# Two halves of queries instead of one block: the score, exp and value steps of an attention loop in a fused transformer block

## The reference

```python
Q, K = _rope(Q, K)
K = jnp.repeat(K, G, axis=1)
V = jnp.repeat(V, G, axis=1)
scores = jnp.einsum('bhqd,bhkd->bhqk', Q, K) / np.sqrt(HD)
w = jax.nn.softmax(scores, axis=-1)
attn = jnp.einsum('bhqk,bhkd->bhqd', w, V)
...
x = x + _L0_attn_ref(xn, ...) + _L0_ffn_ref(xn, ...)
```

## Time and profile before

| | |
|---|---|
| Time, median of 3 runs | 4692.35 us (4692.27 to 4919.59) |
| Time of the profiled execution | 4691.55 us |
| Its span on the slowest core (core 2) | 4690.0 us |
| Spans of the eight cores | 4655.5 to 4690.0 us |
| TensorE busy | 3501.9 us (75% of the span) |
| ScalarE busy | 1244.2 us (27%) |
| VectorE busy | 902.2 us (19%) |
| First and last exp of the attention start at | 1219.7 and 3020.2 us |

### The profile page before, as it was taken

The page is one execution under the profiler, slowest core; times in us unless marked ns, Lnnn a source line. Parts: engine busy times, 40 slices in busy tenths (PEclk is TensorE's granted clock), DMA queues, the critical chain, the costliest instruction groups (busy, mean ns, idle before and its releaser), DMA issues.

```text
span 4690.0 us, 35554 instructions; the slowest of 8 cores (4655.5 to 4690.0 us)
## 1 busy us (share of the span) xinstructions
PE 3501.9 (75%) x13728; PEld 1223.5 (26%) x13898; DVE 902.2 (19%) x1009; ACT 1244.2 (27%) x1100; POOL 224.4 (5%) x428
## 2 busy tenths in 40 slices
PE   3646555555777777777777777759998895999898
PEld 0212111111211111111111111124443342444344
DVE  3242333333111111111111111120000002000000
ACT  1010111111455555555555555500000000000000
POOL 0000000000000000000000000001110000111000
PEclk9878766666888888888888888879999997999999
DMA  5242443433000000000000000079998877999887
GB/s 104 41 90 50 75 87 84 83 79 79 5 0 0 0 0 0 0 0 0 0 0 0 0 0 0 1 143 153 152 150 156 161 142 143 152 153 152 158 161 142
DMA packets 95332, 340.02 MB, mean 72 GB/s; under 512 B 10784, under 2 KB 10816, under 8 KB 90688
## 3 DMA queue, kind: packets, MB, share of 16 engines
q0 software_dynamic: 60608, 274.81, 35.4%
q1 hardware_dynamic: 34560, 62.93, 4.6%
HBM read 604.07 MB, written 8.39 MB: 131 GB/s over the span
## 4 chain that ended last, share of the span: by engine, by line
PE 46%; ACT 22%; DVE 13%; DMA 12%; issue 5%; DVEq 0%; POOL 0%; ACTq 0%; another core or an unknown queue 0%; SPq 0%; POOLq 0%
ACT ptab L450 20%; PE pb L604 9%; PE pb L594 9%; PE pb L438 6%; DMA wo_sb<-wo_t 6%; PE pb L295 6%; PE pb L641 6%; DMA xf_sb<-x_t 3%; PE pb L347 3%; DVE rz_sb L499 2%; DVE rz_sb L501 2%; PE pb L636 2%; DMA xf<-x_t 1%; DVE scrf L273 1%; DVE xt_sb L276 1%
## 5 line engine op out<-in xcount | busy, mean ns | idle before, releaser
L450 ACT ACTIVATE ptab<-pb,negb_sb 128x2048 bf16<-128x2048 f32 x512 | 1007.1, 1967 | 795.3 <-PE pb L438 795.3
L594 PE MATMUL pb<-xt,wg_sb 128*128 128x512 bf16 x2008 | 471.0, 382 | 99.6 <-DVE xt L575 56.6
L438 PE MATMUL pb<-qt_all,kt_all 64*128 64x512 bf16 x2048 | 328.7, 396 | 211.5 <-ACT ptab L450 210.8
L604 PE MATMUL pb<-xt,wu_sb 128*128 128x512 bf16 x2006 | 464.2, 382 | 2.6 <-issue 0.2
L641 PE MATMUL pb<-gated,wd_sb 128*128 128x512 bf16 x2009 | 445.2, 379 | 2.1
L476 PE MATMUL pb<-ptab,v_all 128*64 128x512 bf16 x1024 | 420.8, 411 | 3.0 <-DVE pb L423 3.0
L482 PE MATMUL pb<-ptab,ones_bf 128*1 128x512 bf16 x1024 | 392.3, 383 | 0.0
L610 ACT ACTIVATE silu_sb<-pb 128x512 bf16<-128x512 f32 x128 | 76.4, 597 | 1182.9 <-PE pb L594 1182.8
L499 DVE RECIPROCAL rz_sb<-pb 1x1024 f32<-1x1024 f32 x16 | 104.8, 6551 | 1431.1 <-PE pb L482 1431.1
L295 PE MATMUL pb<-xt_sb,wk_sb 128*128 128x512 bf16 x496 | 204.4, 545 | 213.4 <-DVE xt_sb L276 212.9
L463 PE MATMUL pb<-ptab,v_all 128*65 128x512 bf16 x1024 | 327.2, 402 | 6.0 <-ACT ptab L450 6.0
(11 more groups left out here) (97 smaller groups left out, 1840.2 us busy)
## 6 DMA issues: line engine op xcount, KB each, us to landing
wg_sb<-wg_t POOLq DMA_DIRECT2D x128, 512.0 KB, 6.4
wu_sb<-wu_t POOLq DMA_DIRECT2D x128, 512.0 KB, 6.4
wd_sb<-wd_t POOLq DMA_DIRECT2D x32, 2048.0 KB, 16.0
xf_sb<-x_t SPq DMA_DIRECT2D x128, 256.0 KB, 2.7
xt_sb<-x_t POOLq DMA_DIRECT2D x32, 512.0 KB, 16.0
wk_sb<-wk_t POOLq DMA_DIRECT2D x32, 512.0 KB, 6.9
wq_sb<-wq_t POOLq DMA_DIRECT2D x32, 512.0 KB, 5.5
wo_sb<-wo_t POOLq DMA_DIRECT2D x32, 512.0 KB, 19.5
```

The source lines that it names most:

```text
L438: last = em.emit("tensor", (lambda p, j, c, h, base, off: lambda t: t.matmul(pscore[:, off:off + 512], kt_all[base:base + 64, 4096 * p + 1 ...
L450: exp_ab[c] = em.emit("scalar", (lambda par: lambda s: s.activation(ptab[:, 2048 * par:2048 * (par + 1)], pscore[:, :], AF.Exp, bias=negb_ ...
L594: mg = em.emit("tensor", (lambda par, dc: lambda t: t.matmul(pg[par][:, :], wg_sb[:, 2048 * par + 128 * dc:2048 * par + 128 * (dc + 1)], x ...
L604: mu_ = em.emit("tensor", (lambda par, dc: lambda t: t.matmul(pu[par][:, :], wu_sb[:, 2048 * par + 128 * dc:2048 * par + 128 * (dc + 1)], ...
```

## The change

The unit of the loop becomes one half of the queries (`h`) of a chunk, for both heads. `S_half(c, h)` issues two matmuls, one for each head, into a half of `pscore`, and waits for the exp of the same half of the chunk before. `EXP(c, h)` handles 128 x 1024 scores. `AV(c, h)` issues one A, one B and one O. To keep the two heads of one half side by side, the columns of `pscore` and `ptab` are laid out half first, head second, instead of head first. The tokens `exp_ab`, `s_ab`, `av_a`, `av_b` and `prev_pair_exp` are kept for each half. The end of a pair is as before, except that the first reciprocal names one token, where it named two.

```diff
-        def S_quad(c):
-            w_s = [a_ready, a_ready_sc, negb_tok, exp_ab.get(c - 1)]
+        if j == 0:
+            prev_pair_exp = {}
+
+        def S_half(c, h):
+            w_s = [a_ready, a_ready_sc, negb_tok, exp_ab.get((c - 1, h))]
             if j > 0 and c == 0:
-                w_s.append(prev_pair_exp)
+                w_s.append(prev_pair_exp.get(h))
...
-                    base = 64 * hh
-                    off = 1024 * hh + 512 * h
...
+            for hh in range(2):
+                base = 64 * hh
+                off = 1024 * h + 512 * hh
...
+                    waits=(w_s if hh == 0 else []),
+                    inc=(S_PE if hh == 1 else None))
+            s_ab[(c, h)] = last
+
+        def EXP(c, h):
             par = c % 2
-            w_e = [s_ab[c], av_b.get(c - 2)]
-            exp_ab[c] = em.emit("scalar", (lambda par: lambda s: s.activation(
-                ptab[:, 2048 * par:2048 * (par + 1)], pscore[:, :], AF.Exp,
-                bias=negb_sb[:, :], scale=0.125))(par), waits=w_e, inc=S_SC)
-
-        def AV(c, hh):
+            w_e = [s_ab[(c, h)], av_b.get((c - 2, h))]
+            exp_ab[(c, h)] = em.emit("scalar", (lambda par, h: lambda s: s.activation(
+                ptab[:, 2048 * par + 1024 * h:2048 * par + 1024 * (h + 1)],
+                pscore[:, 1024 * h:1024 * (h + 1)], AF.Exp,
+                bias=negb_sb[:, :], scale=0.125))(par, h), waits=w_e, inc=S_SC)
+
+        def AV(c, h):
...
+            pt_a = ptab[:, 2048 * par + 1024 * h:2048 * par + 1024 * h + 512]
+            pt_b = ptab[:, 2048 * par + 1024 * h + 512:2048 * par + 1024 * (h + 1)]
+            w_av = [exp_ab[(c, h)]]
+            if first and h == 0:
+                w_av.append(prev_evac)
+            av_a[(c, h)] = em.emit("tensor", (lambda c, p, h, first, last, pt_a: lambda t: t.matmul(
+                pava[0:65, 512 * h:512 * (h + 1)],
...
+            w_b = [bmemset] if (first and h == 0) else []
...
+            av_b[(c, h)] = em.emit("tensor", (lambda c, h, pt_b: lambda t: t.matmul(
+                pavb[0:1, 512 * h:512 * (h + 1)], ones_bf[:, 0:1],
+                pt_b, start=False, stop=False, skip_group_check=True))(c, h, pt_b),
+                inc=S_PE)
 
         for c in range(NKCH):
-            S_quad(c)
-            EXP(c)
-            if c >= 1:
-                AV(c - 1, 0)
-                AV(c - 1, 1)
+            for h in range(2):
+                S_half(c, h)
+                EXP(c, h)
+                if c >= 1:
+                    AV(c - 1, h)
         AV(NKCH - 1, 0)
         AV(NKCH - 1, 1)
-        av_final = av_b[NKCH - 1]
-        prev_pair_exp = exp_ab[NKCH - 1]
+        av_final = av_b[(NKCH - 1, 1)]
+        prev_pair_exp = {h: exp_ab[(NKCH - 1, h)] for h in range(2)}
...
-                     waits=[av_a[NKCH - 1], av_final])
+                     waits=[av_final])
```

More of the change, by code:

```diff
@@ L427, in build_nc @@
         s_ab = {}
-        def S_quad(c):
-            w_s = [a_ready, a_ready_sc, negb_tok, exp_ab.get(c - 1)]
+        if j == 0:
+            prev_pair_exp = {}
+        def S_half(c, h):
+            w_s = [a_ready, a_ready_sc, negb_tok, exp_ab.get((c - 1, h))]
             if j > 0 and c == 0:
-                w_s.append(prev_pair_exp)
+                w_s.append(prev_pair_exp.get(h))
             last = None
-            for h in range(2):
-                for hh in range(2):
-                    base = 64 * hh
-                    off = 1024 * hh + 512 * h
[L438 to L445, removed]
@@ L447, in EXP @@
-        def EXP(c):
-            par = c % 2
-            w_e = [s_ab[c], av_b.get(c - 2)]
-            exp_ab[c] = em.emit("scalar", (lambda par: lambda s: s.activation(
-                ptab[:, 2048 * par:2048 * (par + 1)], pscore[:, :], AF.Exp,
-                bias=negb_sb[:, :], scale=0.125))(par), waits=w_e, inc=S_SC)
-        def AV(c, hh):
+            for hh in range(2):
+                base = 64 * hh
+                off = 1024 * h + 512 * hh
+                last = em.emit("tensor", (lambda p, j, c, h, base, off: lambda t: t.matmul(
+                    pscore[:, off:off + 512],
+                    kt_all[base:base + 64, 4096 * p + 128 * c:4096 * p + 128 * (c + 1)],
+                    qt_all[base:base + 64, TOK * j + 512 * h:TOK * j + 512 * (h + 1)],
+                    start=True, stop=True))(p, j, c, h, base, off),
+                    waits=(w_s if hh == 0 else []),
+                    inc=(S_PE if hh == 1 else None))
@@ L455, in AV @@
+            s_ab[(c, h)] = last
+        def EXP(c, h):
+            par = c % 2
+            w_e = [s_ab[(c, h)], av_b.get((c - 2, h))]
[4 more added lines that the diff above has]
+        def AV(c, h):
             par = c % 2
             first, last = (c == 0), (c == NKCH - 1)
[L457 to L487, removed]
@@ L489, in build_nc @@
-        for c in range(NKCH):
-            S_quad(c)
-            EXP(c)
-            if c >= 1:
-                AV(c - 1, 0)
-                AV(c - 1, 1)
+            pt_a = ptab[:, 2048 * par + 1024 * h:2048 * par + 1024 * h + 512]
[5 more added lines that the diff above has]
+                pava[0:65, 512 * h:512 * (h + 1)],
+                v_all[:, VST * c + 65 * (2 * p):VST * c + 65 * (2 * p) + 65],
+                pt_a, start=first, stop=last))(c, p, h, first, last, pt_a),
+                waits=w_av, inc=None)
@@ new lines, in AV @@
+            w_b = [bmemset] if (first and h == 0) else []
+            em.emit("tensor", (lambda c, p, h, pt_b: lambda t: t.matmul(
+                pavb[64:128, 512 * h:512 * (h + 1)],
+                v_all[:, VST * c + 65 * (2 * p + 1):VST * c + 65 * (2 * p + 1) + 64],
+                pt_b, start=False, stop=False, skip_group_check=True))(c, p, h, pt_b),
+                waits=w_b)
+            av_b[(c, h)] = em.emit("tensor", (lambda c, h, pt_b: lambda t: t.matmul(
+                pavb[0:1, 512 * h:512 * (h + 1)], ones_bf[:, 0:1],
+                pt_b, start=False, stop=False, skip_group_check=True))(c, h, pt_b),
+                inc=S_PE)
@@ L495, in build_nc @@
+        for c in range(NKCH):
+            for h in range(2):
[3 more added lines that the diff above has]
+                    AV(c - 1, h)
         AV(NKCH - 1, 0)
         AV(NKCH - 1, 1)
-        av_final = av_b[NKCH - 1]
-        prev_pair_exp = exp_ab[NKCH - 1]
+        av_final = av_b[(NKCH - 1, 1)]
+        prev_pair_exp = {h: exp_ab[(NKCH - 1, h)] for h in range(2)}
+        av_a_final = av_a[(NKCH - 1, 1)]
         q1 = em.emit("vector", lambda v: v.reciprocal(rz_sb[0:1, 0:TOK], pava[64:65, :]),
-                     waits=[av_a[NKCH - 1], av_final])
+                     waits=[av_final])
```

## The result

| | before | after |
|---|---|---|
| Median of all runs | 4692.31 us (10 runs, 4688.08 to 4949.49) | 4622.6 us (8 runs, 4603.7 to 4895.95) |
| Ratio after to before | | 0.9839, 95% interval 0.9818 to 0.986 |
| Span of the profiled execution | 4690.0 us | 4608.6 us |

The change makes the kernel 1.6% faster; 2.6% was forecast.

A forecast was written before the change was run, and what follows sets the result against it. Alternating exp and S were taken as the bound; afterwards a pair's 80.5 us plus clock gives 81.8 instead of 89.4, saving 7.6 us in 16 pairs, 122 us: 4570 us, 2.6% less. Range 4550 to 4595, reaching upward to 4620.

The forecast's parts named there:

- The bound before and after: Attention loop: alternating exp and S bound it, 2.82 us a chunk; afterwards TensorE would, at 2.54 us.
- The exp of the half: ScalarE's exp of 1024 columns, read from a straight line between two sizes: 1.11 us, bounds 0.687 and 1.967.
- The cover over ScalarE's extra work: Two half exps cost ScalarE 0.26 us more a chunk, 133 us in all, hidden behind TensorE.
- The ring: One half's S, exp and next S: 1.74 us must fit into 2.54, so S finds its exp done.
- The half on TensorE: Four steps of TensorE for one half, S to A, A to B, B to O, O to S: 1.27 us.
- The step A to B: TensorE, from the second A's start to B's start, inside each half: 0.31 us.
- The clock: Start of a pair, TensorE at the 1.2 GHz level: 1.1 us lost plus 0.2 for a later rise.
- wait at S: Rival: a satisfied wait costs, say, 0.07 us at each half, 68 us in all, 4638 us; chance 0.12.
- The late clock: Rival: clock stays low 10 us longer in each pair, 3.8 us each, 61 us, 4631 us; chance 0.05.
- The full emptying: Rival: TensorE empties at each change between S and the rest, 269 us slower than now, 4961 us; chance 0.04.
- the first two rivals: A satisfied wait costing at each half's S (4638 us, 0.12) and a clock staying low longer (4631 us, 0.05).
- The clock's rival: After a pair's start the clock stays low 10 us longer, 61 us in all, 4631 us; chance 0.05.

The follow-up runs named there:

- e2: Kernel before the change, with B and O of the second head merged into one matmul: ratio to before 0.9929, 4664.6 us.
- e1: Changed kernel with B and O of the second head merged into one matmul of 65 columns: ratio to before 0.9164, about 4300 us.
- e4: Changed kernel put back to the order of before, all four S ahead, but with two half-size exps: ratio to before 1.0181, 4779.2 us.
- e9: Changed kernel with extra matmuls in every idle stretch of TensorE around a pair's end: 4645.87 us profiled; pairs with the clock at 1.00 from 82.1 us.
- e6: Changed kernel with both halves of chunk 1's S ahead of the wait for the clearing of `pb3`: ratio to before 0.9803.
- e3: Changed kernel with B, B, O, O of both halves grouped at the chunk's end, six changes of matmul kind instead of eight: ratio 0.958, 4501.26 us.
- e5: Changed kernel with 60 extra matmuls at the end of each pair, beside VectorE's reciprocals: ratio to before 0.978.

## Why the prediction was right and wrong

*The bound before and after: right.* The turn of ScalarE and TensorE was the bound (e2), the change undid it, and TensorE took its place (e1). The chain, the idle times and the clock of 1.00 in mid-pair are as forecast.

*The exp of the half: right.* The straight line through two sizes gave 1.114 us and 1114 ns were measured. The cover over ScalarE's extra work was there, and e4 shows the price without it: 85 us, not 133, since two queued exps overlap and take 2.12 us, not 2.23.

*The ring: right.* No S in mid-pair waits for its exp; TensorE's idle time at S lies at the starts of the pairs.

*The half on TensorE: the term that was mis-sized.* I took 1.27 us, and it is 1.298. The step A to B was read from the second A of a run, 0.309 unrounded; in the new order A itself stands behind a change, and the step is 0.335. The other three came out as read: S to A, from the first S of the couple, 0.320 for 0.322, B to O 0.334 for 0.334, O to S 0.309 for 0.310. The unrounded starts behind the rows add to 1.275, and taking 1.27 dropped the rest. The prediction had seen that steps with a change are dearer, but it priced each step by the pair of neighbours, when part of the cost hangs on the neighbour before that. 61 x 0.028 = 1.7 us a pair, 27 us in all. The rounded rows, which add to 1.29, would have come closer than the finer starts.

*The clock: the other mis-sized term.* I allowed 1.3 us a pair, and it is 2.2 (e9): 0.9 more, 14 us in all. I had added 0.2 for a later rise; it came at 5.1 us after the clearing, where 3 had been taken. With both a pair is 82.1 + 2.2 = 84.3 us, as measured, and the two, 2.6 us together, explain the whole distance from 7.6 to 5.1 us a pair. This divides up the measured pair. It does not say that a shorter half would have given its 1.7 us back in full: after a shorter pair the clock may rise later, as in e6.

*The rivals.* No wait at S took anything: O to S is 0.309 us, where it was 0.310 with one wait for four S. The late clock did happen, at a quarter of its price. The full emptying did not: the rule of the Trainium skill ("TensorEngine Tiling (Array Packing)", Key Properties), that changing the tiling mode drains TensorE, is borne out only as 0.11 us a change (e3). A full drain, as I had priced it, would have made the steps O to S and S to A 0.52 us, and they are 0.31 and 0.32. It was right in kind all the same: 0.87 of the 2.59 us of a chunk are such changes, and e3 took two of the eight away for about 120 us ((0.9839 - 0.958) x 4692). It was the largest thing in the changed kernel that the order could still alter, and I had treated it as a remainder.

*The result lies on the other side of 2%.* I gave 0.21 to that. The margin was 28 us on the 122 forecast, and the two terms above take 41. By the ratio the time is 0.9839 x 4692 = 4617 us: outside the forecast's own 4550 to 4595, and inside 4620 only because the range was stretched toward the first two rivals. The clock's rival did take its part; the larger part, the half, was in no rival, and more than the 0.02 us of rounding that the range allowed.

## What to carry to other kernels

When a wait is removed by cutting work into halves, count the changes of matmul shape (rows, columns, place in the array) that the new order makes, price each (0.11 us in this loop), and try the order that groups equal ones. Price a step by a run of matmuls in which the one before it also stands as it will. And before removing a turn between two engines, compute which engine's work bounds it next: the merge of B and O was worth 33 us ahead of this change and 317 behind it.

## What the runs showed of the hardware that was not expected

- Queued exps on ScalarE overlap: two of 1.11 us take 2.12 us (e4), three 3.15 us (e1). The Trainium skill ("ScalarE: Activation LUTs", What ACT_TABLE_LOAD costs) gives about 93 ns for this. The traces agree with about 0.10 us in e4, and show a little more, 0.12, in e1, where exps start 0.997 us apart. I had not used it.
- The end of a pair and the clock hold each other. In e6 less work stood behind the clearing, and the low level lasted 0.9 us longer, so that a pair took the same 84.3 us. A saving of some tenths at such a place can vanish. That the later rise follows from the shorter pair was not tested. It did not swallow a larger saving: e3 kept 6.8 us a pair.
- The clock can fall while TensorE is busy with the fp32 spreading matmuls (one row by 64 columns). In e5 TensorE had stood idle 1.8 us ahead of them, so that e5 alone does not show it. In e9, on core 0, it had not: from 1863 on the spreading matmuls and the extra ones ran in turns without a gap, and the clock fell at 1867.7.

```profile
1863.00:1867.70 4.70, 4.70 (x15) 1.10 (x14) 0.84 (x1) 0.00 (x0) 0.00 (x0) 1.00 0.00 0
1867.70:1871.00 3.30, 3.30 (x6) 0.59 (x4) 0.00 (x0) 0.00 (x0) 0.00 (x0) 0.50 0.00 0
```

In most of e9's pairs it held through the same sequence. What about these matmuls lets it fall was not tried by itself.
